# A gated low-rank layer and a sign matmul on one Trainium2 core: h transposed by SBUF-to-SBUF transfers and VectorE blocks, with a lag of three tiles

## What is computed

```python
base = jnp.einsum('btd,od->bto', x, W)
logits = jnp.einsum('btd,ed->bte', x, Wr) + 5.0 * one_hot(language_ids, 8)
topw, topi = jax.lax.top_k(logits, 2)
weights = jax.nn.softmax(topw, axis=-1)
gates = jnp.sum(one_hot(topi, 8) * weights[..., None], axis=-2)
h = jnp.einsum('btd,erd->bter', x, A)            # 8 experts x 16 = 128 columns
lora_out = jnp.einsum('bter,bte,eor->bto', h, gates, B)
cond = base + 2.0 * lora_out
out = x + jnp.einsum('bsi,io->bso', cond, sign) * jax.nn.softplus(scale)
```

## Time and profile before

| | |
|---|---|
| median of 3 runs | 165.22 us (165.18 to 166.31) |
| profiled execution | 165.43 us, its span 163.6 us |
| PE busy | 158.8 us (97%), 1070 matmuls |
| DVE busy | 98.8 us (60%) |
| ACT busy | 65.9 us (40%) |
| POOL busy | 53.7 us (33%) |
| granted PE clock | 9 tenths or more in all 40 slices |
| DMA | 29431 packets, 19.51 MB, mean 119 GB/s |

### The profile page before, as it was taken

One profiled execution on the slowest core, in us unless ns is written; L12 is line 12 of the kernel. 1 busy time (PEld: TensorE's weight loads), 2 busy tenths in 40 slices (PEclk: granted clock), 3 DMA queues, 4 the chain that ended last, 5 costly groups with the idle time before them and its releaser, 6 DMA issues.

```text
span 163.6 us, 3711 instructions
## 1 busy us (share of the span) xinstructions
PE 158.8 (97%) x1070; PEld 153.7 (94%) x1070; DVE 98.8 (60%) x416; ACT 65.9 (40%) x176; POOL 53.7 (33%) x51
## 2 busy tenths in 40 slices
PE   7999997999999999999999999999999999999993
PEld 5688887999999999999999999999999999999992
DVE  5999967565666655555555555566655555455741
ACT  3644642434443333444443433443333444443340
POOL 2992765222223333333333222223333333333000
PEclk9999999999999999999999999999999999999999
DMA  5993424233333333333333333333333333111113
GB/s 179 380 140 75 132 65 127 69 110 130 118 127 112 126 118 126 128 128 128 128 124 97 105 119 115 116 121 121 119 117 127 128 128 128 64 64 64 68 66 128
DMA packets 29431, 19.51 MB, mean 119 GB/s; under 512 B 7248, under 2 KB 24432, under 8 KB 29424
## 3 DMA queue, kind: packets, MB, share of 16 engines
q1 hardware_dynamic: 28704, 18.25, 36.5%
q10 hardware_dynamic: 720, 1.18, 1.9%
HBM read 11.03 MB, written 8.39 MB: 119 GB/s over the span
## 4 chain that ended last, share of the span: by engine, by line
PE 81%; DVE 12%; DMA 3%; ACT 1%; issue 1%; ACTq 0%; DVEq 0%
PE pair L627 65%; PE pair L644 14%; DMA sign_in<-in_L_ffn_sign 3%; DVE w_lo L427 2%; PE p_ht L651 2%; DVE xt L437 2%; DVE wide_lo L488 1%; DVE sign_hi L442 1%; DVE m_full L484 1%; ACT wide_hi L373 1%; DVE second L535 1%; DVE top_no L530 1%; DVE b_lo L497 0%; DVE wide_lo L477 0%; ACT b_hi L380 0%
## 5 line engine op out<-in xcount | busy, mean ns | idle before, releaser
L304 POOL TENSOR_TENSOR xt_lo<-xt,xt_hi 128x512 fp32r<-128x512 f32 x32 | 41.1, 1286 | 90.0 <-ACT xt_hi L355 89.9
L627 PE MATMUL pair<-wide_hi,xt_hi 128*128 128x392 f32 (+1 forms) x256 | 62.8, 321 | 0.2 <-POOL xt_lo L304 0.2
L627 PE MATMUL pair<-wide_hi,xt_lo 128*128 128x392 f32 (+1 forms) x256 | 60.1, 311 | 0.0
L627 PE MATMUL pair<-wide_lo,xt_hi 128*128 128x392 f32 (+1 forms) x256 | 60.1, 311 | 0.0
L627 PEld LDWEIGHTS pair<-wide_hi,xt_hi 128*128 128x128 f32 x256 | 39.6, 189 | 0.8 <-POOL xt_lo L304 0.5
L627 PEld LDWEIGHTS pair<-wide_hi,xt_lo 128*128 128x128 f32 x256 | 39.8, 188 | 0.0
L627 PEld LDWEIGHTS pair<-wide_lo,xt_hi 128*128 128x128 f32 x256 | 39.7, 188 | 0.0
L399 ACT ACTIVATE y<-pair 128x256 f32<-128x256 f32 x31 | 11.9, 385 | 44.3 <-PE pair L644 44.3
L512 DVE TENSOR_TENSOR logits<-pair,bias 128x8 f32<-128x8 f32 x32 | 5.3, 165 | 35.6 <-PE pair L627 35.6
L437 DVE STREAM_TRANSPOSE xt<-x_in 128x512 f32<-128x512 f32 x32 | 22.7, 710 | 3.7 <-DVE top L520 3.2
L355 ACT ACTIVATE xt_hi<-xt 128x512 fp32r<-128x512 f32 x32 | 20.3, 635 | 2.6 <-DVE xt L437 2.6
(11 more groups left out here) (76 smaller groups left out, 137.0 us busy)
## 6 DMA issues: line engine op xcount, KB each, us to landing
x_in<-in_x SPq DMA_DIRECT2D x128, 64.0 KB, 1.9
out<-y SPq DMA_DIRECT2D x31, 256.0 KB, 2.1
sign_in<-in_L_ffn_sign ACTq DMA_DIRECT2D x4, 256.0 KB, 5.1
w_in<-in_L_cond_W SPq DMA_DIRECT2D x4, 256.0 KB, 4.6
a_in<-in_L_cond_A SPq DMA_DIRECT2D x4, 64.0 KB, 5.0
b_in<-in_L_cond_B SPq DMA_DIRECT2D x4, 64.0 KB, 4.3
out<-y SPq DMA_DIRECT2D x1, 128.0 KB, 1.7
out<-y ACTq DMA_DIRECT2D x1, 128.0 KB, 1.8
```

Source lines behind the costliest of these rows:

```text
L304: nc.gpsimd.tensor_tensor(xt_lo[n][:, :, :].rearrange("p j (g b) -> p g j b", g=NQ), xt[n][:, :, :, :], xt_hi[n][:, :, :].bitcast(FP32).re ...
L627: last = nc.tensor.matmul(pair[n][bank][:, at0:at0 + hi - lo], l[:, k, :], w[:, k, lo:hi], start=(opens and k == 0 and l is xt_hi[n] and w ...
```

## The change

The transpose of the gated h no longer goes through TensorE and PSUM for tiles 0 to 28. Four DMAs (`move_h`, on SyncE's queue) copy blocks of 32 columns of h_gated to four groups of 32 partitions of a new tile h_moved, in pieces of 128 bytes. VectorE then transposes 32x32 blocks of h_moved into ht (`turn_h` on VectorE), ScalarE makes ht_hi from ht, and VectorE makes ht_lo from ht and ht_hi, now from two tensors in SBUF. Tiles 29 to 31 keep the transpose of TensorE, into banks of pairs that are free by then.

The correction of a step now belongs to tile s-3 (LAG=3), and all rings have four buffers instead of three (RING=4, S3=3 before). Four pairs fill the PSUM, so p_ht and p_b2 lose their own banks. Two of the four loads of x of a tile are issued by SyncE and two by ScalarE, and they run four tiles ahead. The loop has four steps a turn, and four turns: steps 7 to 22.

```diff
-        h_gated = sb("h_gated", [P, ER])
+        h_gated = [sb(f"h_gated{n}", [P, ER]) for n in range(RING)]
+        h_moved = [sb(f"h_moved{n}", [P, NQ, Q]) for n in range(RING)]
+        ht = sb("ht", [ER, NQ, Q])
...
         pair = [[ctx.enter_context(nc.psum_tensor(f"pair{n}{k}", [P, 512], FP32)) for k in range(2)]
-                for n in range(S3)]
-        p_ht = ctx.enter_context(nc.psum_tensor("p_ht", [P, 512], FP32))
-        p_b2 = ctx.enter_context(nc.psum_tensor("p_b2", [P, 512], FP32))
+                for n in range(RING)]
+        p_b2 = pair[3][0]
         p_m = [pair[1][0], pair[1][1], pair[2][0], pair[2][1]]
+        p_ht = {TILES - 3: pair[(TILES - 1) % RING][1], TILES - 2: pair[(TILES - 4) % RING][0],
+                TILES - 1: pair[(TILES - 4) % RING][1]}
...
             for i in range(NQ):
                 sp_eng.dma_start(wr_in[Q * i:Q * i + E, :], wr_load[i, :, :]).then_inc(wr_loaded, 16)
             sp_eng.dma_start(ids_in[:, :], lang_ids.rearrange("(p a) -> p a", a=1)).then_inc(ids_loaded, 16)
-            for t in range(1, S3):
+            for t in range(1, RING):
                 load(0, t, t)
 
+            def move_h(q, r, d):
+
+                n = slot(r, d)
+                sp_eng.wait_ge(h_gated_made, RING * q + r + d + 1)
+                for i in range(NQ):
+                    sp_eng.dma_start(h_moved[n][Q * i:Q * i + Q, :, :], h_gated[n][:, Q * i:Q * i + Q])\
+                        .then_inc(h_arrived[n], 16)
+
             def turnover(q, r, s):
 
-                if s is None or s + S3 < TILES:
-                    sp_eng.wait_ge(xt_made, S3 * q + r + 1)
-                    load(q, r, S3 * q + r + S3)
+                if s is None or 0 <= s - LEAD - 1 < LATE:
+                    move_h(q, r, -LEAD - 1)
+                if s is None or s + RING < TILES:
+                    sp_eng.wait_ge(xt_made, RING * q + r + 1)
+                    load(q, r, RING * q + r + RING, NQ // 2)
...
+            def load(q, r, d):
+
+                n = slot(r, d)
+                act.wait_ge(xt_made, RING * q + r + d + 1 - RING)
+                for i in range(NQ // 2, NQ):
+                    act.dma_start(x_in[n][Q * i:Q * i + Q, :, :], x_load[i, :, RING * q + r + d, :, :])\
+                        .then_inc(x_loaded[n], 16)
+
+            load(1, 0, 0)
             for t in range(1, LEAD):
                 high_x(0, t, 0, first=True)
+                load(1, t, 0)
...
+            def high_h(done, late):
+
+                if late is None:
+                    act.wait_ge(ht_made, done - LAG + 1)
+                    nc.scalar.activation(ht_hi[:, :].rearrange("p (b g) -> p g b", g=NQ), ht[:, :, :], ACT.Copy)\
+                        .then_inc(ht_hi_made, 1)
+                else:
+                    act.wait_ge(ht_turned, late - LATE + 1)
+                    act.wait_ge(y_summed, late)
+                    nc.scalar.activation(ht_hi[:, :], p_ht[late][:, 0:P], ACT.Copy).then_inc(ht_hi_made, 1)
+
             def step(q, r, s):
-                if has(s, -LAG):
-
-                    act.wait_ge(ht_turned, S3 * q + r - LAG + 1)
-                    nc.scalar.activation(ht_hi[:, :], p_ht[:, 0:P], ACT.Copy).then_inc(ht_hi_made, 1)
+                if s is None or 0 <= s - LAG < LATE:
...
+                if has(s, LEAD + RING):
+                    load(q, r, LEAD + RING)
...
-            def low_h(done):
-
-                dve.wait_ge(ht_hi_made, done - LAG + 1)
-                nc.vector.tensor_tensor(ht_lo[:, :], p_ht[:, 0:P], ht_hi[:, :].bitcast(FP32), ALU.subtract)\
-                    .then_inc(ht_lo_made, 1)
+            def low_h(done, late):
+
+                dve.wait_ge(ht_hi_made, done - LAG + 1 if late is None else late + 1)
+                if late is None:
+                    nc.vector.tensor_tensor(ht_lo[:, :].rearrange("p (b g) -> p g b", g=NQ), ht[:, :, :],
+                                            ht_hi[:, :].bitcast(FP32).rearrange("p (b g) -> p g b", g=NQ),
+                                            ALU.subtract).then_inc(ht_lo_made, 1)
+                else:
+                    nc.vector.tensor_tensor(ht_lo[:, :], p_ht[late][:, 0:P], ht_hi[:, :].bitcast(FP32),
+                                            ALU.subtract).then_inc(ht_lo_made, 1)
+
+            def turn_h(q, r, s):
+
+                n = slot(r, -LAG)
+                dve.wait_ge(h_arrived[n], 16 * NQ * (turn(q, r, -LAG) + 1))
+                nc.vector.transpose(ht[:, :, :].rearrange("p g b -> p (g b)"),
+                                    h_moved[n][:, :, :].rearrange("p g c -> p (g c)")).then_inc(ht_made, 1)
...
-                hurry = s is not None and s >= TILES - 1
-                if has(s, -LAG) and not hurry:
-                    low_h(done)
+                if s is None or 0 <= s - LAG < LATE:
+                    turn_h(q, r, s)
...
-                if has(s, -LAG) and hurry:
-                    low_h(done)
+                if s is None or 0 <= s - LAG < LATE:
+                    low_h(done, None)
...
+                        pe.wait_ge(y_copied, done - RING + 1)
+                    if s == RING - 1:
+                        pe.wait_ge(b2_lo_made, 1)
                     for k in range(KC // 2):
                         m_there(s, k)
                         wide(r, [k], BANKS, opens=True)
                 if has(s, -LAG):
 
-                    if s == LAG:
-                        pe.wait_ge(b2_lo_made, 1)
...
-                if has(s, -1):
-                    turn_h(done)
```

```diff
                 wide(before, second, (BANKS[0],)).then_inc(head_ready, 1)
+                pe.wait_ge(y_copied, s - RING + 1)
+                turn_h(s - 2)
+
+                pe.wait_ge(xt_lo_made, s + 1)
+                wide(r, first, (BANKS[0],), opens=True)
+                pe.wait_ge(ht_lo_made, s - 2)
+                lora((s - 3) % RING, (0, 1)).then_inc(y_summed, 1)
+                wide(r, second, (BANKS[0],)).then_inc(head_ready, 1)
+                pe.wait_ge(y_copied, s - 2)
                 turn_h(s - 1)
...
+                wide(before, first, (BANKS[1],), opens=True)
+                pe.wait_ge(ht_lo_made, s - 1)
+                lora((s - 2) % RING, (0, 1)).then_inc(y_summed, 1)
+                wide(before, second, (BANKS[1],))
+                wide(r, range(1), (BANKS[1],), opens=True)
                 pe.wait_ge(ht_lo_made, s)
                 lora(before, (0, 1)).then_inc(y_summed, 1)
-                wide(r, range(1), (BANKS[1],), opens=True)
-                turn_h(s + 1)
+                turn_h(s)
```

More of the change, by code:

```diff
@@ L98, in adaln_ffn_kernel @@
         ln_one = sb("ln_one", [P, 1])
-        x_in = [sb(f"x_in{n}", [P, NQ, P]) for n in range(S3)]
-        xt = [sb(f"xt{n}", [P, NQ, KC, Q]) for n in range(S3)]
-        xt_hi = [sb(f"xt_hi{n}", [P, KC, P], FP32R) for n in range(S3)]
-        xt_lo = [sb(f"xt_lo{n}", [P, KC, P], FP32R) for n in range(S3)]
+        x_in = [sb(f"x_in{n}", [P, NQ, P]) for n in range(RING)]
+        xt = [sb(f"xt{n}", [P, NQ, KC, Q]) for n in range(RING)]
+        xt_hi = [sb(f"xt_hi{n}", [P, KC, P], FP32R) for n in range(RING)]
+        xt_lo = [sb(f"xt_lo{n}", [P, KC, P], FP32R) for n in range(RING)]
         logits = sb("logits", [P, E])
@@ L164, in adaln_ffn_kernel @@
         b2_lo_made = sem("b2_lo_made")
-        x_loaded = [sem(f"x_loaded{n}") for n in range(S3)]
-        y_stored = [sem(f"y_stored{n}") for n in range(S3)]
+        x_loaded = [sem(f"x_loaded{n}") for n in range(RING)]
+        y_stored = [sem(f"y_stored{n}") for n in range(RING)]
         xt_made = sem("xt_made")
@@ L182, in adaln_ffn_kernel @@
         h_gated_made = sem("h_gated_made")
+        h_arrived = [sem(f"h_arrived{n}") for n in range(RING)]
+        ht_made = sem("ht_made")
         ht_turned = sem("ht_turned")
@@ L400, in step @@
                     nc.scalar.activation(y[n][:, Y0:D], pair[n][1][:, 0:D - Y0], ACT.Copy).then_inc(y_copied, 1)
+                if s == TILES - 1:
+                    high_h(s, LATE)
                 if has(s, LEAD):
-                    high_x(q, r, LEAD, first=(s is not None and s + LEAD < S3))
+                    high_x(q, r, LEAD, first=(s is not None and s + LEAD < RING))
+                if has(s, LEAD + RING):
+                    load(q, r, LEAD + RING)
             steps(act, step)
             act.wait_ge(y_copied, TILES)
-            act.dma_start(out[:, TILES - 1, Y0:D], y[(TILES - 1) % S3][:, Y0:D])\
-                .then_inc(y_stored[(TILES - 1) % S3], 16)
+            act.dma_start(out[:, TILES - 1, Y0:D], y[(TILES - 1) % RING][:, Y0:D])\
+                .then_inc(y_stored[(TILES - 1) % RING], 16)
         @block.vector
@@ L522, in step @@
                 if has(s, LEAD):
[L523 removed]
+                    turn_x(q, r, LEAD, first=(s is not None and s + LEAD < RING))
                 if has(s, -1):
                     nc.vector.max_index(top_at[:, :], top[:, :], logits[:, :]).then_inc(top_at_made, 1)
[L526 to L527 removed]
```

(30 more changed lines are left out.)

90 lines of the change are left out of this document (49 added, 41 removed).

## The result

| | before | after |
|---|---|---|
| median of four runs each | 165.44 us (165.18 to 166.31) | 172.25 us (171.5 to 172.75) |
| profiled execution, its span | 165.43, 163.6 | 171.5, 169.4 |
| ratio after/before | | 1.039 (1.035 to 1.043) |
| PE busy | 158.8 us (97%), 1070 matmuls | 161.8 us (96%), 1041 matmuls |
| DVE busy | 98.8 us | 104.4 us |

The change makes the kernel 3.9% slower. The direction of the forecast was right, but its 1.5% and its range (up to 169.8) were too low: in the profiled spans +5.8 us against a forecast of +2.55.

A forecast was written before the change was run, and what follows sets the result against it. TensorE bounds the kernel and would wait for ht_lo behind VectorE's longer order. Transposes -3.5, plain steps +1.1, loop +3.9, end +0.8, start +0.25 sum to +2.55: 168.0 us, or 167.8 from the median; range 163.5 to 169.8.

The forecast's parts named there:

- L: The start of a step's logits on VectorE, from which the prediction measures all times in that step, in us.
- Rivals 1 and 2: ht_lo just in time, 164.7 us, chance 0.20; VectorE's order no bound at all, 162.5 us, chance 0.13.
- Rival 4: In each step ht_lo waits for GpSimd's xt_lo; 0.2 us beyond gives 173 us; chance 0.05.
- ht_lo 0.27: VectorE's subtraction making ht_lo, last in its order of a step, was to take 0.27 us, from 0.25 to 0.29.
- the transpose's removal: 29 transposes of h leave TensorE, 0.12 us of its issue each, 3.5 us in all.
- register waits: In the loop, waits on values computed from its counter ahead of VectorE's transposes: 0.16 plus 0.37 us a turn.
- +1.1: At the start, tile 0's block transpose and correction come late: 1.0 us, plus 0.1 for xt_lo of tile 2.
- the end: In the last two steps the correction was to be 0.4 us late, twice: 0.8, with 0.4 and 1.2 as ends.
- 3.2 of 4.37 us: Time SyncE's queue was to spend per step issuing four moves, two loads and a store, against the forecast step.
- cover of 2.5 us: In later steps, the last move of h was to land 2.5 us before the block transpose wants it.
- Rival 3: The moves of h land late and steps follow SyncE's queue: at 0.5 us beyond, 180 us; chance 0.04.
- landing time: A move of h_gated was to land 1.9 us on, if it is like a load of x.

## Why the prediction was right and wrong

**Right: what TensorE waits for.** The bound, its cause and its place were as forecast: idle time that ends with ht_lo, in all 29 steps, larger in the last and the first step of a turn, with ht_lo at L+1.35 (forecast 1.37) and the next logits 2.69 behind the correction (2.68). The correction without a wait comes at L+1.59 (forecast 1.58), as two experiments show. The experiment with ht_lo in front removed the wait, and the one on the kernel before showed that the late place is harmless alone. Rivals 1 and 2, a just-in-time ht_lo and no bound at all, are out. Rival 4 is out too: xt_lo kept its place and ends at L+0.88, ahead of ht_lo, which takes 273 ns there once its stride is gone.

**Wrong: the duration of ht_lo.** The failed term is "ht_lo 0.27", with 0.25 to 0.29 as ends, taken from two rows with dense operands. The diff's rearrangement, which writes every fourth element, was in plain sight and was not priced. It took 0.375, and 0.273 when the experiment took the stride away. Also the transpose's removal is worth 0.08 a step (4.38 to 4.30) and not 0.12, for behind a correction without a wait come 2.71 and not 2.68. A plain step was forecast at 4.37 and is 4.46: over 26 steps 26x0.09=2.3 us more. The register waits cost 0.42 a turn instead of 0.53, over four turns 0.4 less. Together the steps from tile 3 to 29 were to cost 1.9 and cost 3.74. TensorE's wait in a plain step was forecast at 0.11, with 0.16 as its upper end, and is 0.18 to 0.19.

**Wrong: the start.** The term "+1.1" took 0.46 for the issue of a move, the price of a load of x. Four took 2.62, so the last was issued at about 30.25 and not 29.7, and it was there 2.3 later, not 1.9; the transpose of tile 0 came at 32.59 instead of 31.6. The logits of tile 3 stand at 36.85 where the working gives 33.1+2.68=35.8, 1.07 more. The 2.54 of idle time at 34.16 looks worse than that, but 0.5 of it was there only because TensorE had run ahead of VectorE.

**Too small: the end.** 0.4 was forecast twice and 0.62 came, for ScalarE's strided copy took 0.43 instead of 0.28 and ht_lo 0.39 instead of 0.27. On the path that is only 0.2 more than forecast: two steps of 3.53 took 3.06 and 2.98 before, 1.02 more against the 0.8. In sum 1.85+1.07+0.2=3.1 of the 3.25 that the span is above the forecast.

**Wrong, and not visible in the result: "3.2 of 4.37 us" for SyncE's queue.** Its round is 4.3 to 4.7, since a move costs 0.60 and each group comes 0.1 to 0.4 behind the last. So the cover of 2.5 us of the moves shrank to about 1 us where their lag was longest. Rival 3 is false for this kernel, whose only wait for h_moved is that of the start, but it is the next bound: it took the gain of two experiments, and with both bounds mended every step fell to 4.30 in one trace. The landing time was right: 1.9 at the median, like a load of x, though the pieces are 128 bytes. By the Trainium skill, "DMA: Bandwidth & Descriptors", "Why small descriptors are slow (HBM only)", traffic from SBUF to SBUF is free of the penalty of small pieces, and this agrees.

**What stays open.** The medians differ by 6.8 and the spans of the profiled runs by 5.8; the kernels with moves scatter more from run to run (171.5 to 173.0 in eight runs of after). The clock is not it, since it was granted in full (0.998 to 1.0) in all eight. What varies from trace to trace is how late the weights land in the start (L of the first tile by 1 us and more) and single slow issues, on SyncE's queue and on ScalarE's; for one kernel these two explain a span 4.6 longer, but both traces of after are of its faster runs, so for it this is not shown. Why some issues take 1 us or more was not settled. That GpSimd's xt_lo held the first tile's small VectorE instructions rests on their common ends in 14 traces, and on the instruction that is short wherever no xt_lo runs at the same time; no experiment moved xt_lo of tile 2.

## What to carry to other kernels

A unit of work taken from the bound engine pays only what one step of it gets shorter (here 0.08 of 4.38 us), so first follow every input of its next instruction through the engine that takes the work over; if that chain has less slack than it grows by, the change loses. Price an instruction by a row with the same access pattern, not only the same shape. Add up a DMA queue's issues per step by their own kind, with the gaps, and when two chains are nearly as long as the step, expect that mending one shows the other.

## What the runs showed of the hardware that was not expected

- **A stride of 16 bytes in SBUF costs small instructions over a third.** VectorE's subtraction of 128 fp32 columns took 375 ns with it and 273 without, ScalarE's copy 435 and 312.
- **The issue of a DMA has its own price for each form.** On one queue a move from SBUF to SBUF of 16 KB took 0.60 us, a load of 64 KB 0.42, a store of 256 KB 0.38. Seven of them fill a step of 4.46, though the DMA engines are busy for under half of the time.
- **An idle spell can cost twice.** After TensorE sat idle for 2.13 to 2.67 us in the start, the granted clock fell to the 1.2 GHz level in four profiled runs, and in three of them the half step behind it took 1.5 us more; in three others, with 2.34 to 2.54 us idle, it did not. Which of the two it will be can't be told from these rows.
- **A separate wait on a computed value costs 0.09 to 0.16 us** on VectorE in front of the next instruction, 0.19 with a register operation behind it, and shows in the trace as idle time with a releaser that had long been done.
- **GpSimd can hold small VectorE instructions.** A CAST of 128x2 took 0.89 to 1.00 us instead of 0.12 to 0.17, and a TENSOR_SCALAR of 128x8 1.20 to 1.22 instead of 0.28 to 0.29, where a GpSimd subtraction of 128x512 ran at the same time; both ended with it. Transposes and MAX8 beside such a subtraction kept their usual times (0.71 and 0.13 at 78 us of after).
- **An engine's own DMA issues delay its instructions.** Two issues on ScalarE's queue took 2.79 us once, and the activation behind them started at L+2.21 instead of L+0.54.
